# M's scale from a bound on its factors, Wv turned by DMA, two tiles of x turned by TensorE: a two-layer graph kernel on one core

## The chip, the cores and the metric

One core of a Trainium2 chip. The metric is the device time of one execution, in microseconds (us), the median of several runs. Times in the profile are counted from the start of the profiled execution's span.

## The reference, cut to what matters

```python
def reference(x, adj, Wq, bq, Wk, bk, Wv, bv, W1, b1, W2, b2):      # x 4096x512, adj 4096x4096, W* 512x512, W1 512x128
    q, k, v = x @ Wq.T + bq, x @ Wk.T + bk, x @ Wv.T + bv
    a = q @ k.T / sqrt(512) + adj + adj
    x = layernorm(x + softmax(a) @ v)
    h = relu(adj @ (x @ W1) + b1)
    return layernorm(x + adj @ (h @ W2) + b2)
```

## The kernel before, in words

All large products run on TensorE in fp16, each operand split in two: `hi` is the scaled value rounded to fp16 (on ScalarE), `lo` is what is left (on VectorE, `minus_hi`, L1159). A product of two split operands takes three matmuls per block of 128, hi x hi, hi x lo and lo x hi (`terms`, L577, lines 578 to 580), each with 512 columns. The scales are powers of two, taken from maxima or sums of absolute values: VectorE reduces along the free axis, GpSimd takes the maximum over the 128 partitions (`partition_all_reduce`), VectorE rounds to a power (`power`, `scale_of`: four small instructions).

The queries and keys are folded into one matrix. M = Wq' Wk (512 x 512) is made first, in fp32 (line 601), in four PSUM banks `m_bank`. Then the logits are x M x' plus biases: `queries(n)` (L634) makes a 128 x 512 piece of g = M'x' and `values(t)` (L620) a 128 x 512 tile of v. Their order on TensorE is written out at L653 to L662: queries(0) to (3), values(0) to (3), then two of each in turn up to t = 31. Only then come the logits, the softmax and the attention (L665 on, 256 steps of 24 matmuls), and the two convolutions with adj. The change touches nothing of these.

What stands ahead of queries(0), by engine:

- SyncE (SP) issues the loads: the first quarters of Wq and Wk (`d_w0`), their other three (`d_wr`), x group 0 (four tiles of 128 rows, 1 MB), Wv, x group 1. Then it waits, tile by tile, for the split of x and issues a DMA transpose for each of tiles 0 to 3 (`transpose_x`, L362; 256 KB, an fp16 pair, into `xT`), then bv's row, x groups 2 and 3, the transposes of tiles 4 to 7, and x groups 4 to 7. Its waits hold everything behind them.
- TensorE runs nine warm-up matmuls (L595), M (16 products, two instructions each, quarter e = 0 of the weights first), four column sums (L607), c0 (L609), the bias row (L610: ones x part_u, 512 columns, fp32), and 16 transposes of Wv's blocks into PSUM (`wv_transposes`, L588 to L591). queries(0) waits for the four DMA transposes and, block by block, for M's split (`a_m`, `v_m`).
- ScalarE sums |x| of the first half of group 0 (`group_sum`, L849), splits tiles 0 to 3 (`xt_hi`, L858), sums group 1, copies the bias row out of bank 7 (L898, `a_bias`), and makes `m_hi` (L865), `g_hi(0)` (L875) and `wv_hi` (L889) from PSUM.
- VectorE makes `part_u` and `part_g` (`partial`, L1163: Wq's and Wk's rows weighted with the biases), the other half of group 0's sum (L1240), x's scale (`x_scale(0)`, L1186), `xt_lo` (L1182) of tiles 0 to 3, then the maxima over M's banks as they come (`m_max`, L1174), M's scale, the first part of Wv's maximum, `m_lo` (L1208), `g_scale(0)` (L1200), the rest of Wv's maximum, x's second scale, Wv's scale, `wv_lo` (L1178) and the split of tiles 4 to 7.
- GpSimd does the all-reduces in a fixed order (L1572 on) and counts them in `g_ar`.

After that, `g_hi`/`g_lo` scale and split each query piece, `v_full` (L1212), `v_hi` and `v_lo` each tile of v, and `query_bias` (L1280) multiplies x with the bias row. queries(4) to (7) take the banks of queries(0) to (3) again, values(4) to (7) those of values(0) to (3), so they wait for `a_gf` and `v_vf`. The list `x_tiles_at` (L97) says at which tile t the split of a later group of four tiles stands.

## Time and profile before

| | us |
|---|---|
| median of 3 runs | 1907.52 (1907.30 to 1907.54) |
| the profiled execution's own time | 1907.61 |
| its span, first to last instruction | 1905.8 |
| TensorE busy in the span | 1897.2 |
| VectorE, ScalarE, GpSimd busy | 1082.8, 857.4, 116.0 |
| granted TensorE clock, whole span | 1.00 |

The own time is what the device reports for the profiled execution; the span is shorter, as it leaves out what lies before the first and behind the last instruction. Matmuls overlap each other in the profile (each is shown with about 0.38 us, a new one starts every 0.22 us), so starts tell more than durations.

### The profile page before, as it was taken

Reading aid. Unit: us, or ns where it says so; the run is one execution under the profiler, and the core shown is the slowest. Engines: PE = TensorE matmul, PEld = TensorE weight load, DVE = VectorE, ACT = ScalarE, POOL = GpSimd, SP = SyncE. Lnnn points to the kernel's source line nnn. Section 1 sums busy time; section 2 is a strip of 40 time slices with the busy share of each in tenths; the row PEclk is TensorE's granted clock in tenths of the full one; section 3 lists DMA queues with packets and bytes.
Section 4 is the critical chain, followed back from the end, with each engine's and each line's share of the span. In section 5 each row is a group of like instructions: output and inputs, shape, how many; then the busy total and the mean of one; then the engine's idle time right before and its main releaser. Section 6 shows DMA issues by size and latency. Waiting matters only on the chain.

```text
span 1905.8 us, 26547 instructions
## 1 busy us (share of the span) xinstructions
PE 1897.2 (100%) x9273; PEld 889.8 (47%) x9273; DVE 1082.8 (57%) x2107; ACT 857.4 (45%) x1838; POOL 116.0 (6%) x210
## 2 busy tenths in 40 slices
PE   9999999999999999999999999999999999999998
PEld 4444444444444444444444444444444454444446
DVE  7786666666666666666666666666666620001334
ACT  5654455555555455555555555555545611010112
POOL 0000000000000000000000000000000000002334
PEclk9999999999999999999999999999999999999999
DMA  7665599999999999999999999999999999989996
GB/s 234 164 138 123 127 231 227 225 231 227 227 223 226 228 229 228 227 224 226 225 230 225 229 226 231 226 222 226 228 222 237 215 349 387 387 307 358 395 394 244
DMA packets 798903, 463.21 MB, mean 243 GB/s; under 512 B 644656, under 2 KB 652592, under 8 KB 798768
## 3 DMA queue, kind: packets, MB, share of 16 engines
q1 hardware_dynamic: 790704, 447.51, 93.4%
q10 hardware_dynamic: 8064, 14.00, 2.0%
q8 instruction: 73, 1.20, 0.3%
q14 instruction: 62, 0.51, 0.1%
HBM read 220.99 MB, written 92.01 MB: 164 GB/s over the span
## 4 chain that ended last, share of the span: by engine, by line
PE 98%; DVE 1%; DMA 0%; issue 0%; POOL 0%; SPq 0%; ACT 0%; POOLq 0%; DVEq 0%; ACTq 0%
PE bank L578 15%; PE bank L580 15%; PE bank L579 15%; PE bank L690 12%; PE bank L691 12%; PE bank L692 12%; PE bank L814 5%; PE bank L813 5%; PE bank L815 5%; DMA adj_in<-in_L_gnn_Wk 0%; PE bank L777 0%; PE bank L774 0%; PE bank L773 0%; PE bank L834 0%; PE bank L835 0%; PE bank L836 0%
## 5 line engine op out<-in xcount | busy, mean ns | idle before, releaser
L959 ACT ACTIVATE tsp<-ring,sc 128x512 f16<-128x512 f32 x248 | 179.0, 722 | 599.3 <-DMA tsp<-tsp 598.5
L1341 DVE SCALAR_TENSOR_TENSOR ring<-bank,sc,adj_in 128x512 f32<-128x512 f32 x256 | 192.2, 751 | 396.1 <-PE bank L580 391.1
L578 PE MATMUL bank<-xT,gT 128*128 128x512 f16 x1024 | 388.1, 379 | 0.0
L579 PE MATMUL bank<-xT,gT 128*128 128x512 f16 x1024 | 388.1, 379 | 0.0
L580 PE MATMUL bank<-xT,gT 128*128 128x512 f16 x1024 | 388.1, 379 | 0.0
L690 PE MATMUL bank<-xv,tsp 128*128 128x512 f16 x1008 | 382.0, 379 | 0.0
L691 PE MATMUL bank<-xv,tsp 128*128 128x512 f16 x1008 | 382.0, 379 | 0.0
L692 PE MATMUL bank<-xv,tsp 128*128 128x512 f16 x1008 | 382.0, 379 | 0.0
L1160 DVE SCALAR_TENSOR_TENSOR tsp<-adj_in,s_a,tsp 128x512 f16<-128x512 f32 x248 | 184.7, 745 | 48.3 <-ACT tsp L967 47.9
L1160 DVE SCALAR_TENSOR_TENSOR tsp<-ring,sc,tsp 128x512 f16<-128x512 f32 x248 | 184.8, 745 | 0.1
L947 ACT ACTIVATE ring<-ring,bias 128x512 f32<-128x512 f32 x256 | 180.9, 707 | 7.4 <-DVE bias L1358 7.4
L1349 DVE TENSOR_REDUCE r_max<-ring 128x1 f32<-128x512 f32 x256 | 175.7, 686 | 8.8
L967 ACT ACTIVATE tsp<-adj_in,s_a 128x512 f16<-128x512 f32 x248 | 175.1, 706 | 3.9 <-DMA tsp<-tsp 3.6
L935 ACT ACTIVATE junk<-adj_in 128x512 fp8e4<-128x512 f32 x256 | 157.0, 613 | 10.1 <-DMA adj_in<-in_adj 10.0
L579 PEld LDWEIGHTS bank<-xT,gT 128*128 128x128 f16 x1024 | 100.2, 98 | 120.8
L578 PEld LDWEIGHTS bank<-xT,gT 128*128 128x128 f16 x1024 | 100.2, 98 | 120.8
L580 PEld LDWEIGHTS bank<-xT,gT 128*128 128x128 f16 x1024 | 100.2, 98 | 120.8
L692 PEld LDWEIGHTS bank<-xv,tsp 128*128 128x128 f16 x1008 | 98.6, 98 | 118.9
L690 PEld LDWEIGHTS bank<-xv,tsp 128*128 128x128 f16 x1008 | 98.6, 98 | 115.3 <-DMA tsp<-tsp 0.5
L691 PEld LDWEIGHTS bank<-xv,tsp 128*128 128x128 f16 x1008 | 98.6, 98 | 114.8
L1503 DVE TENSOR_TENSOR xv<-bank,xv 128x512 f16<-128x512 f32 x8 | 5.5, 691 | 153.2 <-ACT xv L1048 153.2
L1054 ACT ACTIVATE tsp<-tsp,shift,rstd 128x512 f32<-128x512 f32 x31 | 25.2, 813 | 122.5 <-POOL shift L1618 122.4
(261 smaller groups left out, 2167.3 us busy)
## 6 DMA issues: line engine op xcount, KB each, us to landing
adj_in<-in_adj SPq DMA_DIRECT2D x256, 256.0 KB, 3.2
at_dram<-tsp SPq DMA_DIRECT2D x248, 256.0 KB, 3.2
xv<-at_dram SPq DMA_DIRECT2D x54, 1024.0 KB, 14.5
adj_in<-at_dram SPq DMA_DIRECT2D x29, 1024.0 KB, 14.4
xT<-at_dram SPq DMA_DIRECT2D x20, 1024.0 KB, 13.7
xv<-in_x SPq DMA_DIRECT2D x8, 1024.0 KB, 9.9
g_dram<-tsp SPq DMA_DIRECT2D x32, 256.0 KB, 4.0
...
```

What stands on the lines that cost most here:

```text
L578: pe.matmul(dst, ah, bh, start=first, stop=False)
L579: pe.matmul(dst, ah, bl, start=False, stop=False)
L580: return pe.matmul(dst, al, bh, start=False, stop=last)
L690: pe.matmul(dst, ah, vh, start=(kb == 0 and j == 0), stop=False)
L691: pe.matmul(dst, ah, vl, start=False, stop=False)
L692: last = pe.matmul(dst, al, vh, start=False, stop=(kb == KB - 1 and j == TW - 1))
L947: act.activation(p, p, ACT.Exp, bias=bias[:, r % 2:r % 2 + 1], scale=2.0, accum_out=r_sum[:, r % 2, kb:kb + 1]).then_inc(a_exp, 1)
L959: act.activation(p_split(e)[:, 0:BANK], p, ACT.Copy, scale=col[f"p_up{batch(TW * kb)}"]).then_inc(a_p, 1)
L967: act.activation(asp[a % 2][:, 0:BANK], adj_in[:, a % AR, :], ACT.Copy, scale=s_a[:, r:r + 1]).then_inc(a_ah, 1)
L1160: return dve.scalar_tensor_tensor(dst, src, scale, hi, ALU.mult, ALU.subtract)
L1341: dve.scalar_tensor_tensor(t, s_bank[s % S_BANKS][:, :], col[f"k_l{batch(s // KB)}{batch(TW * (s % KB))}"], adj_in[:, s % AR, :], ALU.mult ...
L1349: dve.tensor_reduce(r_max[:, r % 2, kb:kb + 1], ring[:, s % RING, :], AX, ALU.max).then_inc(v_max, 1)
```

## The change

- **M's scale.** Instead of a maximum over the finished M it takes a bound: for each of the 512 rows, the sum of |Wq| times the maximum of |Wk|, and the largest of these. ScalarE makes the row sums (`row_sum`), VectorE the maxima and their product. The scale is `TOP_M / D` over the bound's power instead of `TOP` over the maximum's. For g's own scale a maximum over the hi half of M (`st_mh`) is taken later. m_hi now waits for each bank by itself.
- **Tiles 2 and 3 of x** are transposed by TensorE in fp32, between M's second and third quarters, into banks 4 and 5, and split from there (`xt_hi_pe`, `xt_lo_pe`). Tiles 0 and 1 stay with the DMA (`X_DMA = 2`).
- **Wv** is split from SBUF, into a part of `xT` that is free until the end, and transposed by four DMA transposes ahead of those of tiles 4 to 7, of bv's row and of x groups 3 to 7; x group 2 goes before them. TensorE's 16 transposes go. Wv's scale comes from sums of |Wv| on ScalarE (over each partition's 2048 values); its maximum is taken later, for v's scale (`st_w`).
- **Order.** part_u is completed behind g_scale(0); the bias row's matmul stands between values(2) and values(3), in bank 0; g_hi(0) to (3) stand behind the split of tiles 4 to 7; the split of tiles 8 to 11 stands at t = 2 instead of t = 4, without a g_hi in its middle.

The diff, cut to its core (the counts in other waits on `g_ar` move by one):

```diff
...
 TOP = 2.0 ** 13
+TOP_M = 2.0 ** 14
...
 def x_tiles_at(t):
 
 
-    return list(range(t + XG, t + 2 * XG)) if t % XG == 0 and 0 < t < NT - XG else []
+    if t == XG - 2:
+        return list(range(2 * XG, 3 * XG))
+    return list(range(t + XG, t + 2 * XG)) if t % XG == 0 and XG < t < NT - XG else []
 
...
-        wv_bank = bank[4:8]
+        wv_split = xT[:, KB - 1, :, :, :].rearrange("p two k n -> p (two k n)").rearrange("p (k two d) -> p k two d", k=KD, two=2)
+        row_sums = c_all[:, 0:KD]
 
         def queries_bank(n):
...
-            for t in range(XS):
+            for t in range(X_DMA):
+                transpose_x(t)
+            load_x(X_FIRST)
+            for k in range(KD):
+                sp.wait_ge(a_wv, k + 1)
+                sp.wait_ge(v_wv, k + 1)
+                sp.dma_start_transpose(wvT.rearrange("p two k e -> p (two k) e")[:, :, P * k:P * (k + 1)],
+                                       wv_split[:, k, :, :].rearrange("p two d -> p (two d)")).then_inc(d_wvt, 16)
+            for t in range(XG, 2 * XG):
                 transpose_x(t)
             sp.dma_start(bv_row, bv.rearrange("(o d) -> o d", o=1).broadcast_to([P, D])).then_inc(d_bv, 16)
-            for i in range(X_FIRST, X_FIRST + 2):
-                load_x(i)
-            for t in range(XG, 2 * XG):
-                transpose_x(t)
-            for i in range(X_FIRST + 2, NT // XG):
+            for i in range(X_FIRST + 1, NT // XG):
...
             for t in range(NT):
                 for q in x_tiles_at(t):
+                    if q == NT - XG:
+                        sp.wait_ge(d_wvt, 16 * KD)
                     transpose_x(q)
                 if t == XG:
...
-            def wv_transposes(j):
-                for k in range(KD):
-                    last = pe.transpose(wv_bank[j][:, P * k:P * (k + 1)], wv_raw[:, k, P * j:P * (j + 1)], ident)
-                last.then_inc(p_wv, 1)
+            def x_transposes_first():
+                pe.wait_ge(d_x[0], 16)
+                pe.wait_ge(g_id, 2)
+                for t in range(X_DMA, XG):
+                    for k in range(KD):
+                        last = pe.transpose(x_bank[t - X_DMA][:, P * k:P * (k + 1)], xv[:, t, P * k:P * (k + 1)], ident)
+                    last.then_inc(p_xt, 1)
...
                 if e == 1:
                     pe.wait_ge(d_wr, 16 * 2)
+                if e == 2:
+                    x_transposes_first()
                 for k in range(KD):
                     last = pe.matmul(m_bank[k][:, :], wq_raw[:, e, P * k:P * (k + 1)], wk_raw[:, e, :],
                                      start=(e == 0), stop=(e == KD - 1))
                     if e == KD - 1:
                         last.then_inc(p_pre, 1)
-            pe.wait_ge(v_part, 3)
+            pe.wait_ge(v_part, 2)
...
             last.then_inc(p_pre, 1)
             pe.matmul(bank[6][:, KD:KD + 1], ones, col["c0p"], start=True, stop=True).then_inc(p_pre, 1)
-            pe.matmul(bank[7][:, :], ones, part_u, start=True, stop=True).then_inc(p_pre, 1)
-            pe.wait_ge(d_wv, 16)
-            pe.wait_ge(g_id, 2)
-            wv_transposes(0)
-            wv_transposes(1)
-            pe.wait_ge(v_gb, 2)
-            wv_transposes(2)
-            pe.wait_ge(a_bias, 1)
-            wv_transposes(3)
+
+            def bias_row():
+                pe.wait_ge(v_part, 3)
+                pe.wait_ge(a_gf, 1)
+                pe.matmul(bank[0][:, :], ones, part_u, start=True, stop=True).then_inc(p_pre, 1)
...
             def values(t):
                 if t >= V_BANKS:
                     pe.wait_ge(v_vf, t - V_BANKS + 1)
-                if t % XG == 0:
+                if t == 0:
+                    pe.wait_ge(d_wvt, 16 * KD)
+                elif t % XG == 0:
                     for i in range(XS):
-                        pe.wait_ge(d_xt[i], 16 * (t // XG + 1))
+                        pe.wait_ge(d_xt[i], 16 * x_transposes(t + i))
+                if t == 2:
+                    pe.wait_ge(v_gb, 2)
                 for k in range(KD):
-                    if t == 0:
-                        pe.wait_ge(a_wv, k + 1)
-                        pe.wait_ge(v_wv, k + 1)
                     last = terms(v_bank[t % V_BANKS][:, :], xt_block(0, k, P * t, P), xt_block(1, k, P * t, P),
                                  wvT[:, 0, k, :], wvT[:, 1, k, :], k == 0, k == KD - 1)
                 last.then_inc(p_v, 1)
...
             def queries(n):
                 g, kk = divmod(n, KD)
                 if kk == 0:
+                    if g == 0:
+                        pe.wait_ge(a_xt, XG)
+                        pe.wait_ge(v_xt, XG)
                     for i in range(XS):
-                        pe.wait_ge(d_xt[i], 16 * (g + 1))
+                        if x_transposes(XG * g + i):
+                            pe.wait_ge(d_xt[i], 16 * x_transposes(XG * g + i))
...
                 elif n >= Q_BANKS:
+                    if n == Q_BANKS:
+                        pe.wait_ge(a_bias, 1)
                     pe.wait_ge(a_gf, n - Q_BANKS + 1)
...
             for n in range(XG):
                 queries(n)
-            for t in range(XG):
+            for t in range(XG - 1):
                 values(t)
+            bias_row()
+            values(XG - 1)
...
+            def row_sum(e):
+                if e:
+                    act.wait_ge(a_rs, e)
+                act.activation(x_junk[:, 0:D], wq_raw[:, e, :], ACT.Abs, accum_out=row_sums[:, e:e + 1], saturate=False).then_inc(a_rs, 1)
...
+            def xt_hi_pe(t):
+                act.wait_ge(p_xt, t - X_DMA + 1)
+                act.activation(xt_pe(0, t), x_bank[t - X_DMA][:, :].rearrange("p (k n) -> p k n", n=P), ACT.Identity,
+                               scale=col["s_x0"]).then_inc(a_xt, 1)
...
             def m_hi(k):
+                act.wait_ge(p_pre, k + 1)
                 act.activation(m_hl[:, 0, k, :], m_bank[k][:, :], ACT.Identity, scale=col["s_m"]).then_inc(a_m, 1)
...
             def wv_hi(k):
-                act.wait_ge(p_wv, k + 1)
-                act.activation(wvT[:, 0, k, :], wv_bank[k][:, :], ACT.Identity, scale=col["s_wv"]).then_inc(a_wv, 1)
-
+                act.activation(wv_split[:, k, 0, :], wv_raw[:, k, :], ACT.Identity, scale=col["s_wv"]).then_inc(a_wv, 1)
+
+            act.wait_ge(d_w0, 16 * 2)
+            row_sum(0)
+            act.wait_ge(d_wr, 16 * 2)
+            for e in range(1, KD):
+                row_sum(e)
+            act.wait_ge(a_rs, KD)
             group_sum(0)
-            for t in range(XS):
+            for t in range(X_DMA):
                 xt_hi(t)
-            group_sum(1)
-            act.wait_ge(p_pre, KD + 3)
-            act.activation(c_row, bank[7][:, :], ACT.Copy).then_inc(a_bias, 1)
+            act.wait_ge(d_wv, 16)
+            act.wait_ge(a_xs, 1)
+            act.activation(x_junk[:, 0:KD * D], flat(wv_raw), ACT.Abs, accum_out=col["t1"], saturate=False).then_inc(a_ws, 1)
+            for t in range(X_DMA, XG):
+                xt_hi_pe(t)
             act.wait_ge(v_sm, 1)
             for k in range(KD):
                 m_hi(k)
-            g_hi(0)
             act.wait_ge(v_sc, 1)
             for k in range(KD):
                 wv_hi(k)
+            act.wait_ge(a_ws, 1)
+            group_sum(1)
             for t in range(XG, 2 * XG):
                 xt_hi(t)
-            for n in range(1, XG):
+            group_sum(X_FIRST)
+            for n in range(XG):
                 g_hi(n)
-            group_sum(X_FIRST)
+            act.wait_ge(p_pre, KD + 3)
+            act.activation(c_row, bank[0][:, :], ACT.Copy).then_inc(a_bias, 1)
+            group_sum(X_FIRST + 1)
...
                 for i, q in enumerate(x_tiles_at(t)):
-                    if i == 2:
+                    if i == 2 and t >= XG:
...
-            def wv_max(i, rows):
-                link(abs_max(col[f"t{i}"], flat(wv_raw[:, rows, :])))
-
-            def m_max(k):
-                dve.wait_ge(p_pre, k + 1)
-                link(abs_max(col[f"m{k}"], m_bank[k][:, :]))
...
             def wv_lo(k):
                 dve.wait_ge(a_wv, k + 1)
-                minus_hi(wvT[:, 1, k, :], wv_bank[k][:, :], col["s_wv"], wvT[:, 0, k, :]).then_inc(v_wv, 1)
+                minus_hi(wv_split[:, k, 1, :], wv_raw[:, k, :], col["s_wv"], wv_split[:, k, 0, :]).then_inc(v_wv, 1)
...
+            def xt_lo_pe(t):
+                dve.wait_ge(a_xt, t + 1)
+                hi, lo = (xT[:, 0, part, :, P * t:P * (t + 1)] for part in range(2))
+                minus_hi(lo, x_bank[t - X_DMA][:, :].rearrange("p (k n) -> p k n", n=P), col["s_x0"], hi).then_inc(v_xt, 1)
...
-                link(dve.tensor_scalar(col["k_g"], col[f"e_x{b}"], col["e_m"], LOGIT / TOP ** 2, ALU.mult, ALU.mult))
-                link(dve.tensor_scalar(col["bound"], col["k_g"], 4.0 * TOP ** 2, col["mx_gb"], ALU.mult, ALU.add))
+                link(dve.tensor_scalar(col["k_g"], col[f"e_x{b}"], col["e_m"], LOGIT * D / (TOP * TOP_M), ALU.mult, ALU.mult))
+                link(dve.tensor_scalar(col["bound"], col["k_g"], col["mx_mh"], col["mx_gb"], ALU.mult, ALU.add))
...
             partial(part_g, wk_raw, bq_c, 0)
             link(dve.tensor_tensor(bqk[:, :], bq_c[:, :], bk_c[:, :], ALU.mult))
             dve.tensor_reduce(col["c0p"], bqk[:, :], AX, ALU.add).then_inc(v_part, 1)
+            link(abs_max(col["m0"], wk_raw[:, 0, :]))
             dve.wait_ge(d_wr, 16 * 2)
-            for e in range(1, KD - 1):
-                partial(part_u, wq_raw, bk_c, e)
-                partial(part_g, wk_raw, bq_c, e)
+            link(abs_max(cols("m1", "m3"), wk_raw[:, 1:KD, :]))
+            partial(part_g, wk_raw, bq_c, 1)
             dve.wait_ge(d_x[0], 16)
             dve.tensor_reduce(x_sum[:, 1:2], flat(xv[:, XG // 2:XG, :]), AX, ALU.add, apply_absolute_value=True).then_inc(v_st, 1)
-            partial(part_u, wq_raw, bk_c, KD - 1)
+            partial(part_g, wk_raw, bq_c, 2)
             x_scale(0)
+            dve.wait_ge(a_rs, KD)
+            link(dve.tensor_tensor(cols("m0", "m3"), cols("m0", "m3"), row_sums, ALU.mult))
+            dve.tensor_reduce(col["t0"], cols("m0", "m3"), AX, ALU.max).then_inc(v_st, 1)
+            for t in range(X_DMA):
+                xt_lo(t)
+            dve.wait_ge(g_ar, 2)
+            power(col["e_m"], col["e_m"], TINY_M)
+            scale_of(col["s_m"], col["e_m"], TOP_M / D).then_inc(v_sm, 1)
             partial(part_g, wk_raw, bq_c, KD - 1)
-            for t in range(XG):
-                xt_lo(t)
+            for t in range(X_DMA, XG):
+                xt_lo_pe(t)
+            dve.wait_ge(v_sm, 1)
+            m_lo(0)
+            dve.wait_ge(g_ar, 3)
+            power(col["e_wv"], col["e_wv"])
+            scale_of(col["s_wv"], col["e_wv"]).then_inc(v_sc, 1)
+            for k in range(1, KD):
+                m_lo(k)
+            dve.wait_ge(v_sc, 1)
             for k in range(KD):
-                m_max(k)
-            dve.tensor_reduce(col["st_m"], cols("m0", "m3"), AX, ALU.max).then_inc(v_st, 1)
+                wv_lo(k)
             dve.wait_ge(p_pre, KD + 2)
             dve.tensor_scalar(gb_c[:, :], bank[6][:, 0:KD], LOGIT, None, ALU.mult).then_inc(v_gb, 1)
             dve.tensor_scalar(col["c0"], bank[6][:, KD:KD + 1], LOGIT, None, ALU.mult).then_inc(v_gb, 1)
             dve.wait_ge(v_gb, 2)
-            abs_max(col["st_gb"], gb_c[:, :]).then_inc(v_st, 1)
-            dve.wait_ge(g_ar, 3)
-            power(col["e_m"], col["mx_m"])
-            scale_of(col["s_m"], col["e_m"]).then_inc(v_sm, 1)
-            dve.wait_ge(d_wv, 16)
-            wv_max(0, slice(0, 1))
-            dve.wait_ge(v_sm, 1)
-            for k in range(KD):
-                m_lo(k)
-            dve.wait_ge(g_ar, 4)
-            g_scale(0)
-            wv_max(1, slice(1, KD))
-            dve.tensor_reduce(col["st_wv"], cols("t0", "t1"), AX, ALU.max).then_inc(v_st, 1)
+            link(abs_max(col["st_gb"], gb_c[:, :]))
+            abs_max(col["st_mh"], m_hl[:, 0, :, :].rearrange("p k e -> p (k e)")).then_inc(v_st, 1)
             x_scale(1)
-            dve.wait_ge(g_ar, 5)
-            power(col["e_wv"], col["mx_wv"])
-            scale_of(col["s_wv"], col["e_wv"]).then_inc(v_sc, 1)
-            g_lo(0)
-            dve.wait_ge(v_sc, 1)
-            for k in range(KD):
-                wv_lo(k)
             for t in range(XG, 2 * XG):
                 xt_lo(t)
+            dve.wait_ge(g_ar, 5)
+            link(dve.tensor_scalar(col["mx_mh"], col["mx_mh"], 2.002 * TOP, None, ALU.mult))
+            g_scale(0)
+            for e in range(1, KD):
+                partial(part_u, wq_raw, bk_c, e)
+            g_lo(0)
             g_lo(1)
+            abs_max(col["st_w"], flat(wv_raw)).then_inc(v_st, 1)
             dve.wait_ge(d_bv, 16)
             link(abs_max(col["mx_bv"], bv_row))
-            v_scale(0)
             def query_bias(t):
                 dve.wait_ge(d_x[t // XG], 16)
                 dve.tensor_tensor_reduce(unused, xv[:, t, :], c_row, 1.0, 0.0, ALU.mult, ALU.add, c_all[:, t:t + 1]).then_inc(v_c, 1)
 
             dve.wait_ge(a_bias, 1)
             query_bias(0)
+            dve.wait_ge(g_ar, 6)
+            link(dve.tensor_scalar(col["mx_w"], col["mx_w"], 2.0, None, ALU.mult))
+            v_scale(0)
...
+            pool.wait_ge(v_st, 2)
+            pool.partition_all_reduce(col["e_m"], col["t0"], P, ALL_MAX).then_inc(g_ar, 1)
+            pool.wait_ge(a_ws, 1)
+            pool.partition_all_reduce(col["e_wv"], col["t1"], P, ALL_MAX).then_inc(g_ar, 1)
             pool.wait_ge(a_xs, 2)
             pool.partition_all_reduce(x_all[:, X_COLUMNS[1]], x_sum[:, X_COLUMNS[1]], P, ALL_MAX).then_inc(g_ar, 1)
-            pool.wait_ge(v_st, 2)
-            pool.partition_all_reduce(col["mx_m"], col["st_m"], P, ALL_MAX).then_inc(g_ar, 1)
             pool.wait_ge(v_st, 3)
-            pool.partition_all_reduce(col["mx_gb"], col["st_gb"], P, ALL_MAX).then_inc(g_ar, 1)
+            pool.partition_all_reduce(cols("mx_gb", "mx_mh"), cols("st_gb", "st_mh"), P, ALL_MAX).then_inc(g_ar, 1)
             pool.wait_ge(v_st, 4)
-            pool.partition_all_reduce(col["mx_wv"], col["st_wv"], P, ALL_MAX).then_inc(g_ar, 1)
+            pool.partition_all_reduce(col["mx_w"], col["st_w"], P, ALL_MAX).then_inc(g_ar, 1)
...
```

## Rows read from the trace of the kernel before

**Rows 1.** The page, busy time by engine, share of the span, instructions.

```profile
PE 1897.2 (100%) x9273; PEld 889.8 (47%) x9273; DVE 1082.8 (57%) x2107; ACT 857.4 (45%) x1838; POOL 116.0 (6%) x210
```

**Rows 2.** Busy time by stretch; columns: stretch, length, engines, granted clock, DMA share, GB/s.

```profile
0.00:25.20 25.20, 22.69 (x78) 13.38 (x79) 15.68 (x35) 9.19 (x13) 2.64 (x13) 1.00 0.81 255
25.20:46.00 20.80, 20.79 (x97) 9.24 (x98) 19.72 (x50) 15.87 (x24) 0.75 (x2) 1.00 0.70 200
...
240.00:1500.00 1260.00, 1260.00 (x6097) 581.85 (x6096) 806.99 (x1499) 660.31 (x1506) 40.92 (x60) 1.00 1.02 227
```

**Rows 3.** The chain that ended last, in order of time: start, us, what.

```profile
23.30 0.17 DVE sc L1157
...
24.31 0.76 DVE ring L1160
25.07 0.14 issue
...
224.86 0.39 PE bank L690
```

**Rows 4.** SP's timeline: the first four DMA transposes; and transposes' time to landing.

```profile
17.39 2.71 SPq L366 DMA_TRANSPOSE xT<-ring  x2
20.19 1.29 SPq L366 DMA_TRANSPOSE xT<-x1s  x1
21.57 1.29 SPq L366 DMA_TRANSPOSE xT<-w_hl  x1
...
DMA to landing us min/median/max: 3.1/3.2/3.3
```

**Rows 5.** Timeline of TensorE ahead of queries(0): start, us, line, out<-in.

```profile
9.55 0.30 PEld L601 LDWEIGHTS bank<-adj_in 128*128 128x128 f32 x2 [0.91 <-DMA adj_in<-in_L_gnn_Wk]
...
19.96 0.95 PE L607 MATMUL bank<-tsp 128*128 128x1 f32 x8
...
20.99 1.10 PE L610 MATMUL bank<-tsp 128*128 128x512 f32 x2
21.93 1.91 PE L590 MATMUL bank<-junk,adj_in 128*128 128x128 f32 x16
25.21 0.38 PE L578 MATMUL bank<-xT,ring 128*128 128x512 f16 x1 [1.36 <-DVE ring L1160]
```

**Rows 6.** ScalarE's timeline, ahead of values(0) and, last, in the attention.

```profile
12.27 1.06 ACT L855 ACTIVATE gT<-xv 128x1024 fp8e4<-128x1024 f32 x1 [9.34 <-DMA xv<-in_x]
...
15.79 1.33 ACT L863 ACTIVATE ring<-xv,sc 128x512 f16<-128x512 f32 x2 [2.37 <-DVE sc L1157]
...
18.26 1.89 ACT L855 ACTIVATE gT<-xv 128x2048 fp8e4<-128x2048 f32 x1
...
28.72 0.78 ACT L882 ACTIVATE adj_in<-bank,gb_s,sc 128x512 f32<-128x512 f32 x1 [2.81 <-DVE gb_s L1206]
29.53 0.63 ACT L887 ACTIVATE tsp<-adj_in 128x512 f16<-128x512 f32 x1
...
1002.18 0.61 ACT L935 ACTIVATE junk<-adj_in 128x512 fp8e4<-128x512 f32 x1
```

**Rows 7.** VectorE's timeline in the same stretch.

```profile
12.69 1.22 DVE L1240 TENSOR_REDUCE x_sum<-xv 128x1 f32<-128x1024 f32 x1
...
15.60 0.15 DVE L1157 TENSOR_SCALAR sc<-sc 128x1 f32<-128x1 f32 x1
...
24.31 2.73 DVE L1160 SCALAR_TENSOR_TENSOR ring<-bank,sc,ring 128x512 f16<-128x512 f32 x4 [0.26 <-ACT ring L866]
...
26.95 0.20 DVE L1201 TENSOR_SCALAR sc<-sc 128x1 f32<-128x1 f32 x1
...
28.54 1.75 DVE L1149 TENSOR_REDUCE sc<-adj_in 128x1 f32<-128x1536 f32 x1
```

**Rows 8.** GpSimd's timeline: the first all-reduce.

```profile
14.13 0.67 POOL L1572 PARTITION_ALL_REDUCE x_all<-x_sum  x1 [12.18 <-DVE x_sum L1240]
```

**Rows 9.** DMA issues in 16 to 27 us: KB each, median us to landing.

```profile
xv<-in_x SPq DMA_DIRECT2D x2, 1024.0 KB, 8.8
```

More of the change, by code:

```diff
@@ L22 @@
 XS = 4
+X_DMA = 2
 X_FIRST = 2
@@ L46 @@
 TOP = 2.0 ** 13
+TOP_M = 2.0 ** 14
 TINY = 2.0 ** -40
+TINY_M = 2.0 ** -62
 EXP_BITS = 0x7F800000
@@ L215, in gnn_program @@
         minus_mean = sb("minus_mean", [P, O_RING], F32)
-        names = ["m0", "m1", "m2", "m3", "st_wv", "st_w1", "mx_wv", "mx_w1", "e_wv", "e_w1", "s_wv", "s_w1",
-                 "st_m", "st_gb", "mx_m", "mx_gb", "e_m", "s_m", "mx_bv", "c0p", "c0", "t0", "t1", "u0", "u1", "bound",
+        names = ["m0", "m1", "m2", "m3", "st_w1", "mx_w1", "e_wv", "e_w1", "s_wv", "s_w1",
+                 "st_gb", "st_mh", "st_w", "mx_gb", "mx_mh", "mx_w", "e_m", "s_m", "mx_bv", "c0p", "c0", "t0", "t1", "u0", "u1", "bound",
                  "mx_x", "e_x0", "s_x0", "k_v0", "e_v0", "s_v0", "k_g", "e_g0", "s_g", "k_gs0", "p_up0",
@@ L261, in gnn_program @@
         v_row = [tsp[:, 8, :].bitcast(F32), adj_in[:, 9, :]]
-        g_rows = [adj_in[:, first + i, :] for first in (2, 10) for i in range(2)]
+        g_rows = [adj_in[:, first + i, :] for first in (4, 10) for i in range(2)]
         unused = gT[:, 1, 0:D].bitcast(BF16)
@@ L290, in gnn_program @@
         m_bank = bank[0:4]
+        x_bank = bank[4:6]
         def g_row(n):
@@ L314, in gnn_program @@
             sem(s) for s in ("d_small", "d_bv", "d_w1", "d_b1", "d_wv", "d_late"))
+        d_wvt = sem("d_wvt")
         d_w0, d_wr = sem("d_w0"), sem("d_wr")
@@ L328, in gnn_program @@
         d_out = [sem(f"d_out{i}") for i in range(O_RING)]
-        p_wv, p_pre, p_v, p_g, p_qk, p_pv, p_y, p_adj, p_x1, p_unit, p_h, p_o, p_end = (
-            sem("p_" + s) for s in "wv pre v g qk pv y adj x1 unit h o end".split())
+        p_xt, p_pre, p_v, p_g, p_qk, p_pv, p_y, p_adj, p_x1, p_unit, p_h, p_o, p_end = (
+            sem("p_" + s) for s in "xt pre v g qk pv y adj x1 unit h o end".split())
+        a_rs, a_ws = sem("a_rs"), sem("a_ws")
         a_w2, v_w2, v_z, v_o = sem("a_w2"), sem("v_w2"), sem("v_z"), sem("v_o")
@@ L860, in xt_hi, with xt_pe @@
                     act.wait_ge(v_sx, batch(t) + 1)
-                if t >= XS:
-                    act.wait_ge(d_xt[t % XS], 16 * (t // XS))
+                if t >= XS and x_transposes(t - XS):
+                    act.wait_ge(d_xt[t % XS], 16 * x_transposes(t - XS))
                 act.activation(x_split[t % XS][:, 0:D], xv[:, t, :], ACT.Identity, scale=col[f"s_x{batch(t)}"]).then_inc(a_xt, 1)
+            def row_sum(e):
+                if e:
+                    act.wait_ge(a_rs, e)
+                act.activation(x_junk[:, 0:D], wq_raw[:, e, :], ACT.Abs, accum_out=row_sums[:, e:e + 1], saturate=False).then_inc(a_rs, 1)
+            def xt_pe(part, t):
+                return xT[:, 0, part, :, P * t:P * (t + 1)]
+            def xt_hi_pe(t):
+                act.wait_ge(p_xt, t - X_DMA + 1)
+                act.activation(xt_pe(0, t), x_bank[t - X_DMA][:, :].rearrange("p (k n) -> p k n", n=P), ACT.Identity,
+                               scale=col["s_x0"]).then_inc(a_xt, 1)
             def m_hi(k):
+                act.wait_ge(p_pre, k + 1)
                 act.activation(m_hl[:, 0, k, :], m_bank[k][:, :], ACT.Identity, scale=col["s_m"]).then_inc(a_m, 1)
@@ L920, in _ @@
                 v_hi(t)
-                if X_FIRST + 1 + t < NT // XG:
-                    group_sum(X_FIRST + 1 + t)
+                if 2 <= t < NT // XG - X_FIRST:
+                    group_sum(X_FIRST + t)
             for i in range(XS):
-                act.wait_ge(d_xt[i], 16 * len(range(i, NT, XS)))
+                act.wait_ge(d_xt[i], 16 * x_transposes(NT - XS + i))
             act.wait_ge(v_scales, 1)
@@ L983, in x1_hi @@
                     for i in range(XS):
-                        act.wait_ge(d_xt[i], 16 * len(range(i, NT, XS)))
+                        act.wait_ge(d_xt[i], 16 * x_transposes(NT - XS + i))
                 act.activation(x1s[:, 0:D], xr[:, :], ACT.Copy, scale=X1_UP).then_inc(a_x1, 1)
@@ L1293, in _ @@
                         x_scale(batch(q))
-                    if i == 2:
+                    if i == 2 and t >= XG:
                         g_lo(t)
@@ L1323, in _ @@
                 if t == NT // 2 + 4:
-                    dve.wait_ge(g_ar, 8)
+                    dve.wait_ge(g_ar, 9)
                     power(col["e_w1"], col["mx_w1"])
```

16 lines of the change are left out of this document (9 added, 7 removed).

## The prediction

> **What bounds the kernel now.** I read the busy times by engine first: TensorE is busy for 1897.2 of the span's 1905.8 us [rows 1]. Then the busy time by stretch [rows 2]: in 0 to 25.2 us TensorE has 22.69 us, in 25.2 to 46.0 it has 20.79 of 20.80, in 240 to 1500 it has all of 1260, and the granted clock is 1.00 in each, the 2.4 GHz level. So the only place where a change at the start can win is the idle time and the order of work before the first three-term product, which starts at 25.21. The 20.8 us behind it hold eight products (queries(0) to (3), values(0) to (3)) of twelve matmuls, 2.60 us each; queries(4) starts at 25.21 + 8 x 2.60 = 46.01. That start is the number to predict: from there on the same products follow in the same order.
>
> The chain of waits says what ends last [rows 3]: m_lo(0) on VectorE from 24.31, 0.14 us of issue after its end at 25.07, then queries(0). Behind it stand the four maxima over the M banks, one all-reduce and the scale. But a second wait ends almost together with it: the transposes of x's first four tiles are issued at 17.39, about 18.8, 20.19 and 21.57 and land 3.1 to 3.3 us after issue [rows 4], the last at 21.57 + 3.2 = 24.8. Removing M's maxima alone would win 0.3 us. And TensorE's own queue ends with M's product, four small sums, c0, the bias row and 16 transposes of Wv, from 21.93 for 1.91 us [rows 5]. All three have to move; the change moves all three.
>
> **VectorE and ScalarE ahead of M's scale.** ScalarE gets four row sums of Wq. One costs 0.61 us plus its accumulator read, 0.7 to 0.8 with the wait between (the adj sums in [rows 6] are of that shape). Three follow the weights at 9.55: done by 11.9, ahead of x group 0, which releases ScalarE at 12.27 [rows 6]. So they cost nothing; without that cover each would push s_x0 by 0.8. On VectorE a maximum over 1536 elements (1.75 us [rows 7]) takes the place of two partial sums of 0.76, part_u goes behind, and x_sum can start at 12.3 instead of 12.69 [rows 7]. s_x0, ready at 15.75 before (the multiply at 15.60 is its last step), comes at 15.35 (x_sum to 13.5, 0.2 to GpSimd, all-reduce 0.67 [rows 8], then five small steps of 0.19, the pace of [rows 3]). The product of sums and maxima takes two more small steps; its all-reduce is over by 16.6 and hides beside xt_hi and xt_lo of tiles 0 and 1. xt_lo(1) is done at 17.5 and s_m at 18.2, over 5 us before its old time of 23.45.
>
> ScalarE: xt_hi(0), (1) 15.4 to 16.7 (1.33 for two [rows 6]); the sum over 2048 elements of Wv 16.6 to 18.6 (1.89 + 0.19 read, by group_sum(1)'s row); two PSUM passes for tiles 2 and 3 to 19.9; then m_hi(0), whose bank has been ready since 18.5, 19.8 to 20.5. VectorE: part_g's last term to 18.9, xt_lo_pe of tiles 2 and 3 19.35 to 20.8, m_lo(0) 20.7 to 21.45, four small steps for s_wv to 22.1, m_lo(1), (2), (3) ending at 22.8, 23.45 and 24.1 (0.66 us apart [rows 7]).
>
> **TensorE.** 24 instructions from 9.55 to 19.96 make M's last three quarters, 0.43 us each, 0.87 a product [rows 5]. Eight fp32 transposes now stand inside: 1.91/16 = 0.12 each, 0.95 in all. M ends at 20.9; the sums and c0 take 20.99 - 19.96 = 1.03 as before: free at 21.95. queries(0) also needs m_lo(0) (21.45 + 0.15 = 21.6), xt_lo_pe(3) (20.8) and the DMAs of tiles 0 and 1 (issued at 16.95 and 18.3, landed 21.5). TensorE's own queue ends last, with 0.35 us between the three. Inside queries(0) each quarter takes 0.65, and m_lo(1) at 22.8 + 0.1 holds the second by 0.3; the last starts at 24.2. It ends at 24.87 against 27.83 before: **2.95 us gained**.
>
> **Values.** queries(1) to (3) end at 32.67. values(0) now waits for four DMA transposes of Wv's split. wv_hi runs on ScalarE 22.1 to 24.7, wv_lo on VectorE 24.0 to 26.8, each 0.66 apart, first pair at 24.8. SP waits on each pair; behind it stand x tiles 4 to 7, bv's row and x groups 3 to 7. Issue is at 24.85 and then every 1.38 us (that of [rows 4]): the last at 29.0, landed at 32.2. **0.5 us of slack, the thinnest of the change.** From both sides: with landing at 3.1 and x2 out of the way it is 32.1; if the first Wv transpose finds x group 2 in the queue, it can be late. Group 2 is issued at 19.65; a 1 MB group took 8.8 us to land where two were issued among transposes [rows 9], so 28.5 is the far end. I take 32.2, since only two transposes (to 21.5) stand before a single megabyte.
>
> On that place a rule speaks: the transposes of [rows 4] keep 1.38 us between issues for 256 KB, 190 GB/s. The Trainium skill (Advanced Engine Details and Errata, X-Bar Transpose) says that transposing DMAs are as fast as plain ones, 350 to 400 GB/s. By it, as an estimate from that figure, Wv's four would land at about 30: over 2 us of slack, rival (b) all but gone, the sum the same. The trace disagrees, and I go by the trace.
>
> **The bias row and queries(4).** values(0) to (2) end at 40.47. bias_row, once in the idle stretch, now stands between values(2) and (3): two fp32 instructions, 21.93 - 20.99 = 0.94 us [rows 5], **lost in full**. It waits for part_u and g_hi(0). VectorE after wv_lo: maximum over M's 2048 fp16 (no such row; 1.75 x 2048/1536 = 2.3, from 1.2 if two bytes go twice as fast) to 29.4, s_x1 30.3, xt_lo(4) to (7) to 33.8, g_scale(0) (26.95 to 28.54 is 1.6 [rows 7]) to 35.5, part_u's three terms to 37.8: 2.6 before 40.47. g_hi(0) gives its bank back at 36.5. bias_row ends at 41.4, values(3) at **44.0**. queries(4) needs the copy of the row out of bank 0, on ScalarE behind g_hi(0) to (3): 35.65 + 4 x 1.35 (0.76 + 0.63 [rows 6]), with 0.2 of waiting for g_lo, is 41.2; the row is in by 41.55, copied 42.15, slack 1.8. Tiles 4 to 7 are issued from 31.9 to 36.0 and land at 39.2, slack 4.8.
>
> Next in line is values(4) at 49.2, which wants v_full(0). VectorE: g_lo(1) to 39.1, Wv's maximum 2.3 to 41.4, bv (issued 37.3, 5 us at worst) 42.3 to 43.0, query bias, v_scale(0) 1.3 (six small steps), g_lo(2), v_full(0) done at 46.5: slack 2.7. The third group's split at t = 2 then needs x group 3 (issued 37.9, landed 46.7 by the 8.8 us) and its sum at 48.7; VectorE comes there at 50.6. v_full(2) at 55 for values(6) at 59.6; tiles 8 to 11 land at 60.4 for queries(8) at 64.8. All hidden.
>
> **The sum.** 46.01 - 44.0 = **2.0 us** less: 2.95 gained, 0.94 given back. TensorE has no other waits to take it up: the only odd step later is 0.2 us at 224.86 [rows 3], and everything up to there moves with TensorE. The profiled execution's own time is 1907.61, span 1905.8; the median of the runs is 1907.52. 1907.55 - 2.05 gives **1905.5**.
>
> **The rivals.** (a) The thin waits are late by a little: Wv's transposes, a_bias, or m_lo(1) cost 0.5 to 2 us in all. For it: three starts lie within 0.5 us, and my steps carry 0.1 us errors a dozen times over. Against it: all else has over 1.8. Result 1906.0 to 1907.5. (b) Slower: Wv's transposes queue behind x group 2 at values(0). With group 2 landing at 28.5 the four follow at 1.38, the last landing at 28.5 + 3 x 1.38 + 3.2 = 35.8, 3.1 us after values(0) could start: 1905.5 + 3.1 = 1908.6. It decides from a landing later than 32.67 + 2.0 = 34.7. Against it: alone in the queue a megabyte is through in some 3 us. (c) More gained: M's quarters without the stall of m_lo(1), and the 0.2 us at 224.86 gone: 1905.0. (d) The change doesn't do what it says: s_m late, as the scale waits for row sums or the all-reduce. It has 1.6 us before m_hi(0) wants it, and with the old order of events kept but the bias row and DMA waits added it would be 1907.5 to 1908.5.
>
> **How the numbers follow.** The forecast (1904.9 to 1906.0) 0.60, (a) 0.22, (b) 0.07, (c) 0.06, (d) 0.05. The range of 8 in 10 takes the forecast, (c)'s upper part and (a) up to 1907.1. A measurement of this kernel tells 0.2%, 3.8 us, from no change: faster wants a start of queries(4) before 42.2, which the bias row and TensorE's own queue exclude (0.02). Slower wants the landing of (b) 5.9 us beyond need, or several waits of over 2.6 us (0.04). The rest, 0.94, is within 0.2%.
>
> **What would show it.** In the trace after: the first matmul of queries(0) at 22.0 with next to no idle time before it; 16 transposes gone, eight inside M's product; a gap of 0.3 inside queries(0); none before values(0); the bias row's 0.94 us before values(3); queries(4) at 44.0. Wrong if values(0) shows a DMA wait, if queries(0) starts after 23, or if a gap appears before queries(4) or values(4).

## The result and the profile after

The change makes the kernel **slower by 5.4 us**: 1912.74 us (median of 8 runs, 1912.17 to 1913.86) against 1907.32 (8 runs, 1907.10 to 1907.54), ratio 1.0029, interval 1.0018 to 1.0040. The forecast was 1905.5 and no measurable change. The profiled execution took 1912.83, with a span of 1910.9.

The start of the trace is within 0.3 us of the forecast. TensorE's timeline after, at queries(0), the bias row, queries(4), and at queries(12) (start, us, line, out<-in; an idle time before and its releaser in brackets):

```profile
20.50 0.95 PE L633 MATMUL bank<-tsp 128*128 128x1 f32 x8
21.31 0.36 PE L635 MATMUL bank<-sc,tsp 128*128 128x1 f32 x2
21.61 0.38 PE L599 MATMUL bank<-xT,ring 128*128 128x512 f16 x1
...
40.27 1.02 PE L640 MATMUL bank<-tsp 128*128 128x512 f32 x2
41.13 0.38 PE L599 MATMUL bank<-ring,xT 128*128 128x512 f16 x1
...
43.72 0.38 PE L599 MATMUL bank<-xT,ring 128*128 128x512 f16 x1
...
84.94 0.38 PE L601 MATMUL bank<-ring,xT 128*128 128x512 f16 x1
89.94 0.59 PE L599 MATMUL bank<-xT,ring 128*128 128x512 f16 x1 [4.61 <-ACT adj_in L927]
90.31 0.63 PE L600 MATMUL bank<-xT,ring 128*128 128x512 f16 x1
```

queries(0), the last row of [rows 5], starts at 21.61 instead of 25.21. queries(4) starts at 43.72; the kernel before starts it at 45.96 by the same view, so 2.24 us are won there, and they are still there at 84.94. Then queries(12) starts at 89.94, where 84.94 + 0.22 = 85.16 was due: **4.78 us lost in one wait**. And the matmuls behind it are 0.43 us apart instead of 0.22. Busy time by stretch, in the columns of [rows 2] (TensorE's busy time is the third figure; granted clock, DMA share and GB/s are the last three):

```profile
84.00:86.00 2.00, 1.32 (x7) 0.39 (x4) 2.00 (x4) 0.65 (x2) 0.00 (x0) 1.00 1.04 194
86.00:88.00 2.00, 0.00 (x0) 0.00 (x0) 1.81 (x5) 0.72 (x1) 0.00 (x0) 1.00 0.95 184
88.00:90.00 2.00, 0.07 (x1) 0.10 (x2) 1.71 (x4) 1.58 (x3) 0.00 (x0) 0.53 1.01 205
90.00:92.00 2.00, 2.00 (x5) 0.64 (x6) 0.89 (x2) 1.74 (x3) 0.00 (x0) 0.50 0.94 215
92.00:94.00 2.00, 2.00 (x6) 0.76 (x5) 1.82 (x5) 0.72 (x1) 0.00 (x0) 0.50 0.91 209
94.00:96.00 2.00, 2.00 (x8) 0.79 (x7) 1.96 (x4) 0.61 (x1) 0.00 (x0) 0.76 0.00 0
```

The granted clock goes from 1.00 to 0.50 (2.4 to 1.2 GHz) while TensorE stands still, and the matmuls are 0.22 us apart again from 94.99 on. The twelve starts from 89.94 to the next at 94.99 take 5.05 us instead of 2.59: another 2.46. The account: -2.24 + 4.78 + 2.46 = +5.0; the spans differ by 5.1.

Who is late? The profile puts the wait down to ScalarE's g_hi (L927), but queries(12) also waits for the DMA transposes of tiles 12 to 15. SP's timeline after, and below it what the transposes' own view says of their landing and of who waited:

```profile
82.37 2.63 SPq L381 DMA_TRANSPOSE xT<-ring  x2
85.09 1.29 SPq L381 DMA_TRANSPOSE xT<-x1s  x1
86.47 1.28 SPq L381 DMA_TRANSPOSE xT<-w_hl  x1
```

```profile
  PEld bank L599: 5.1, 1
...
DMA to landing us min/median/max: 3.2/3.2/3.3
```

Tile 15 lands at 86.47 + 3.2 = 89.7, and TensorE starts at 89.94. The same view of the kernel before:

```profile
78.36 2.60 SPq L366 DMA_TRANSPOSE xT<-ring  x2
81.05 1.28 SPq L366 DMA_TRANSPOSE xT<-x1s  x1
82.43 1.29 SPq L366 DMA_TRANSPOSE xT<-w_hl  x1
```

There tile 15 landed at 82.43 + 3.2 = 85.6, and queries(12) started at 87.40: about 1.8 us of slack, at a place that neither the diff nor the waits of TensorE point to. After, TensorE comes 2.24 earlier and the last issue 4.0 later. ScalarE's timeline after shows where most of the 4.0 come from:

```profile
59.70 1.89 ACT L886 ACTIVATE gT<-xv 128x2048 fp8e4<-128x2048 f32 x1
61.50 0.19 ACT L886 ACTIVATION_READ_ACCUMULATOR gT<-xv 128x1 f32 x1
61.59 0.76 ACT L927 ACTIVATE adj_in<-bank,gb_s,sc 128x512 f32<-128x512 f32 x1
...
68.89 1.89 ACT L886 ACTIVATE gT<-xv 128x2048 fp8e4<-128x2048 f32 x1
70.69 0.19 ACT L886 ACTIVATION_READ_ACCUMULATOR gT<-xv 128x1 f32 x1
70.78 0.76 ACT L927 ACTIVATE adj_in<-bank,gb_s,sc 128x512 f32<-128x512 f32 x1
```

and VectorE's, its g_lo at those two places:

```profile
63.12 0.69 DVE L1281 TENSOR_TENSOR tsp<-adj_in,tsp 128x512 f16<-128x512 f32 x1 [1.34 <-ACT tsp L932]
...
72.24 0.69 DVE L1281 TENSOR_TENSOR tsp<-adj_in,tsp 128x512 f16<-128x512 f32 x1 [2.47 <-ACT tsp L932]
```

These are the sums of |x| of x groups 5 and 7. The diff ahead of the prediction does not show the lines that put them there:

```diff
                 v_hi(t)
-                if X_FIRST + 1 + t < NT // XG:
-                    group_sum(X_FIRST + 1 + t)
+                if 2 <= t < NT // XG - X_FIRST:
+                    group_sum(X_FIRST + t)
```

With `X_FIRST` = 2 the sums of groups 4 to 7 move from t = 1 to 4 to t = 2 to 5 (group 3's moves from t = 0 to ahead of the loop). Sums 5 and 7, at t = 3 and t = 5, now stand right ahead of g_hi(4) and g_hi(6). VectorE waits for each g, and the values behind it wait too: v_full(4) starts at 64.98 instead of 62.98, v_full(6) at 74.17 instead of 70.28.

### The profile page after: what moved, and what is told of

It reads as the page before. It is cut to its first block, busy times and chain, and to the rows that moved or that the text cites. A ratio compares the mean times of both kernels' runs of the same rounds, so it can differ in the third digit from the quotient of the medians.

```text
span 1910.9 us, 26546 instructions
## 1 busy us (share of the span) xinstructions
PE 1898.7 (99%) x9265; PEld 889.4 (47%) x9265; DVE 1085.5 (57%) x2107; ACT 862.2 (45%) x1848; POOL 116.4 (6%) x211
## 4 chain that ended last, share of the span: by engine, by line
PE 94%; DVE 2%; ACT 1%; DMA 1%; issue 1%; SPq 0%; POOL 0%; POOLq 0%; DVEq 0%; ACTq 0%
PE bank L599 14%; PE bank L600 14%; PE bank L601 14%; PE bank L721 12%; PE bank L722 12%; PE bank L723 12%; PE bank L845 5%; PE bank L844 5%; PE bank L846 5%; DMA xv<-in_x 0%; PE bank L808 0%; PE bank L805 0%; PE bank L804 0%; PE bank L866 0%; PE bank L865 0%
```

## The experiments

Three theories of why the split of tiles 12 to 15 is late. **A**: these two sums. **B**: the values' chain starts too late (v_full(0) at 45.26 instead of 42.12; bv's row and two maxima over 2048 elements stand ahead of it) and never catches up. **C**: the split of tiles 8 to 11 at t = 2 pushes the later one. And the clock: does it fall because of the wait?

All are edits of the changed kernel. Times are medians of eight to eleven runs, the last two columns are from the one profiled execution (in f_sum7 and e_warm this was the slowest of its ten, at 1910.45 and 1911.76); the kernel before ran beside them at 1907.2. "Last issue" is SP's last transpose of tiles 12 to 15, "idle" TensorE's idle time right before queries(12).

| run | edit | us | last issue | idle |
|---|---|---|---|---|
| the change | | 1912.74 | 86.47 | 4.61 |
| e_sums | sums 4 to 7 at t = 2, 4, 6, 8 | 1906.39 | 82.78 | 0.43 |
| f_sum7 | sum 7 at t = 6 | 1909.65 | 85.09 | 2.33 |
| e_bv | bv's load before Wv's transposes | 1911.98 | 85.53 | 4.18 |
| e_t4 | tiles 8 to 11 at t = 4 | 1910.38 | 86.61 | 0.25, and 2.53 before queries(8) |
| f_t6 | tiles 12 to 15 at t = 6 | 1906.45 | 76.09 | none |
| e_warm | matmuls in the wait | 1910.43 | 87.33 | filled |
| f_best | sums, bv and t = 6 together | 1905.58 | 71.85 | none |

**The sums.**

```diff
-                if 2 <= t < NT // XG - X_FIRST:
-                    group_sum(X_FIRST + t)
+                if t % 2 == 0 and 2 <= t < 10:
+                    group_sum(X_FIRST + 1 + t // 2)
```

> The changed kernel with x's group sums 4 to 7 on ScalarE behind v_hi of t = 2, 4, 6, 8 instead of t = 2, 3, 4, 5. Theory A (the sums at t = 3 and t = 5 stand right ahead of g_hi(4) and g_hi(6), 1.9 us each; VectorE waits for these, and with it the split and the DMA transposes of tiles 12 to 15 come 3.8 us later, behind the start of queries(12)): the last transpose of tile 15 lands near 85.9 instead of 89.7, TensorE waits 1 us or less before queries(12) instead of 4.6, the granted clock stays at 1.00, and the time falls from 1912.7 to 1905.2 to 1906.2. Theory B (the chain of the values starts 3 us too late, bv's load and the two maxima over 2048 elements being in front of it): the wait before queries(12) stays over 3 us and the time over 1911. Theory C (the split of tiles 8 to 11 at t = 2 is what pushes the later one): the same as B.

Measured 1906.39 (1905.98 to 1907.01), ratio to the kernel before 0.9996 (0.9987 to 1.0005). The last issue moves by 3.7 us, as A has it; TensorE waits 0.43 us, and the clock stays up (the second row is a stretch, in the columns of [rows 2]):

```profile
86.17 0.38 PE L599 MATMUL bank<-xT,ring 128*128 128x512 f16 x1 [0.43 <-DMA xT<-w_hl]
...
84.00:88.00 4.00, 3.57 (x18) 1.49 (x16) 2.72 (x6) 3.94 (x7) 0.38 (x1) 1.00 0.98 208
```

Here the wait is named as what it is, the DMA into `xT`. The time is 0.2 us above A's range; this execution also waited 0.50 us for Wv's transposes before values(0). **6.3 us of the change's time hang on where the sums stand.** (The edit also moves sum 6, which stood ahead of no g_hi.) Next, half of the edit, only sum 7 moved:

```diff
-                if 2 <= t < NT // XG - X_FIRST:
-                    group_sum(X_FIRST + t)
+                if t in (2, 3, 4, 6):
+                    group_sum(X_FIRST + min(t, 5))
```

> The changed kernel with only x's group sum 7 moved, from t = 5 (right ahead of g_hi(6)) to t = 6; sums 4, 5 and 6 stay at t = 2, 3, 4. A dose: if each sum that stands right ahead of a g_hi costs 1.9 us, the DMA transposes of tiles 12 to 15 come 1.9 us earlier than in the changed kernel, TensorE waits about 2.7 us before queries(12) instead of 4.6, the clock still falls, and the time is 1910.0 to 1911.5. If the lateness is worked off in another way (both sums together, or the first alone), it is near 1906.4 or 1912.7.

1909.65 (1907.66 to 1910.45): near the range, 0.35 us below it. The last issue came 1.4 us earlier. The idle time fell by 2.3, more than that, as TensorE itself came 0.8 later in this execution (it was idle for 0.73 us ahead of values(0), against 0.16 in the change). The clock still fell to 0.50. Three of the ten runs were at 1907.66, 1907.70 and 1907.96; whether the clock held in these was not profiled.

**The place of the splits.**

```diff
-    if t == XG - 2:
-        return list(range(2 * XG, 3 * XG))
-    return list(range(t + XG, t + 2 * XG)) if t % XG == 0 and XG < t < NT - XG else []
+    return list(range(t + XG, t + 2 * XG)) if t % XG == 0 and 0 < t < NT - XG else []
```

> The changed kernel with the split of tiles 8 to 11 back at t = 4, with g_hi(4) and g_lo(4) in its middle, as in the kernel before. Theory C (the place at t = 2 is to blame): the wait before queries(12) is gone, about 1905. Theory A: g_hi(4) now stands in the middle of the split, where ScalarE's sum of t = 3 is hidden behind x's third scale, so one of the two sums' 1.9 us goes; the other stays: a wait of 2 to 3 us before queries(12), 1908 to 1910. Theory B: little changes, 1911 to 1913. The last transpose of tile 11 must then also land before queries(8) at about 64: 62.85 + 3.2 in the kernel before would be too late by 1 to 2 us for it, a new wait in every theory.

1910.38 (1908.81 to 1911.85). The new wait came, 2.53 us before queries(8), and took the clock down with it:

```profile
67.21 0.58 PE L597 MATMUL bank<-xT,ring 128*128 128x512 f16 x1 [2.53 <-DMA xT<-w_hl]
```

That delay brought TensorE to queries(12) late enough to wait only 0.25 there, although the last issue was at 86.61, no earlier than in the change. So C, which had the wait gone and 1905, falls as the whole cause. But the last issue hides a part of it. The split of tile 15 on VectorE, first in the change, then in e_t4, and SP's first two transposes of the group in e_t4:

```profile
84.14 0.74 DVE L1216 SCALAR_TENSOR_TENSOR w_hl<-xv,sc,w_hl 128x512 f16<-128x512 f32 x1
82.95 0.75 DVE L1214 SCALAR_TENSOR_TENSOR w_hl<-xv,sc,w_hl 128x512 f16<-128x512 f32 x1
81.18 3.95 SPq L379 DMA_TRANSPOSE xT<-ring  x2
```

With the old place VectorE had the split 1.2 us earlier, and SP lost that again: its two issues took 3.95 us instead of 2.63. Why is not known. The place at t = 2 thus has a share of 1.2 us in VectorE's lateness; what it would be worth in time no run shows. The move to t = 2 is still the part of the change that queries(8) needs. A's 2 to 3 us at queries(12) were not seen either, since the loss at queries(8) hid them. The other way round, tiles 12 to 15 earlier as well:

```diff
+    if t in (XG - 2, 2 * XG - 2):
+        return list(range(t + XG + 2, t + 2 * XG + 2))
+    return list(range(t + XG, t + 2 * XG)) if t % XG == 0 and 2 * XG < t < NT - XG else []
```

> The changed kernel with the split and the transposes of tiles 12 to 15 at t = 6 instead of t = 8, g_hi(6) in their middle; the group sums stay where the change has them. If nothing but the landing of tile 15 holds queries(12), it lands some 5 us or more earlier, the wait is gone and the time is 1905.0 (the 2.5 us gained ahead of queries(4) stay, and nothing is lost). If queries(12) is held by something else (the bank's release by g_hi, the profile's ACT L927), the wait stays at over 3 us and the time at 1911 or more.

1906.45 (1906.12 to 1906.82): the wait before queries(12) is gone, so the landing of tile 15 and not the bank held it, and the profile's "ACT adj_in L927" was not the cause. (e_warm below says the same: its extra matmuls also wait for that bank, and start without a gap.) The time is 1.4 us above my figure. Part of that is a wait one group later (tiles 16 to 19 at t = 12, 0.51 us):

```profile
106.54 0.38 PE L599 MATMUL bank<-xT,ring 128*128 128x512 f16 x1 [0.51 <-DMA xT<-w_hl]
```

**bv's row.**

```diff
             load_x(X_FIRST)
+            sp.dma_start(bv_row, bv.rearrange("(o d) -> o d", o=1).broadcast_to([P, D])).then_inc(d_bv, 16)
             for k in range(KD):
...
-            sp.dma_start(bv_row, bv.rearrange("(o d) -> o d", o=1).broadcast_to([P, D])).then_inc(d_bv, 16)
```

> The changed kernel with bv's row loaded right behind x group 2, ahead of Wv's DMA transposes, instead of behind the transposes of tiles 4 to 7. VectorE's wait for it (0.86 us ahead of 41.81) goes. Theory B (the late start of the values' chain sets the lateness at tiles 12 to 15): everything on VectorE from 41.8 on comes 0.9 us earlier, the wait before queries(12) falls from 4.6 to about 3.7 and the time by 0.9 to 2 us. Theory A: VectorE meets the g pieces anyway at t = 4 and t = 6 where ScalarE's sums hold it, so less than 0.5 us is seen.

1911.98 (1911.0 to 1913.02), 0.8 less; the last issue came 0.94 earlier. B's 0.9 us for VectorE is right and A's "less than 0.5" wrong: VectorE does carry a delay from 42 us through to 82. The idle time fell by only 0.43, as TensorE also came 0.44 earlier, and the 0.8 us of time are just under B's range, with the two kernels' runs overlapping (1912.17 to 1913.86 in the change). B's part is 0.9 of lateness, the sums' 3.7, so A is the larger. No run has these two edits alone together; with t = 6 in both, f_best has its last issue 4.2 us ahead of f_t6's, near their sum.

**The clock.**

```diff
+                if n == 3 * XG:
+                    pe.wait_ge(a_gf, n - Q_BANKS + 1)
+                    for _ in range(22):
+                        pe.matmul(queries_bank(n)[:, :], m_hl[:, 0, 0, 0:P], xt_block(0, 0, 0, BANK), start=True, stop=True)
```

> The changed kernel with 22 matmuls of 512 columns on old data in TensorE's queue ahead of queries(12), into the bank that queries(12) overwrites: they only fill the wait (22 x 0.216 = 4.75 us against 5.0 between the starts around it). If the half clock of the first eleven matmuls of queries(12) comes from the wait before it, the clock stays 1.00, these matmuls start every 0.216 us instead of 0.43 and 2.4 us are gained: 1910.2. If the clock fell for another reason (a fixed time, the load), the time stays at 1912.7.

1910.43 (1909.94 to 1911.76), 2.3 less. The matmuls start right behind the last of values, and the clock is 1.00 in the stretch that had 0.50:

```profile
86.52 4.91 PE L662 MATMUL bank<-xT,ring 128*128 128x512 f16 x22
...
88.00:92.00 4.00, 4.00 (x20) 1.84 (x19) 3.25 (x6) 2.69 (x4) 0.00 (x0) 1.00 0.97 200
```

So the wait itself took the clock down, and the loss divides into the 4.8 of the wait and about 2.4 of the clock behind it.

**All repairs, and what each move at the start is worth.** Sums, bv and t = 6 in one kernel:

> All three repairs on the changed kernel: tiles 12 to 15 split at t = 6, the group sums behind even tiles, bv's row loaded ahead of Wv's transposes. Every wait of TensorE behind 22 us should be gone but the 0.3 of the first attention step: 25.2 - 21.6 = 3.6 us gained at the start, 0.9 given to the bias row: 1904.6 to 1905.2, 2.3 us below the kernel before.

1905.58 (1905.17 to 1906.18), ratio to the kernel before 0.9992 (0.9983 to 1.0001); span 1903.6 against 1905.8. No wait of TensorE over 0.4 us is left behind queries(0)'s start. The gain is 1.7 us by medians and 2.2 by spans, a little less than I expected, and within what this measurement can tell from nothing. On this kernel I undid the three moves one at a time. What the three cost (6.5, 5.6 and 1.2 us) does not add up to the gain of 1.7: they work on waits that end together ahead of queries(0), so each alone, undone, holds back the others' gain too, and in two of them the fall of the clock comes on top. M's scale held back until the four maxima over the banks are done (its value stays the bound's):

```diff
-            dve.tensor_reduce(col["t0"], cols("m0", "m3"), AX, ALU.max).then_inc(v_st, 1)
             for t in range(X_DMA):
                 xt_lo(t)
-            dve.wait_ge(g_ar, 2)
-            power(col["e_m"], col["e_m"], TINY_M)
-            scale_of(col["s_m"], col["e_m"], TOP_M / D).then_inc(v_sm, 1)
             partial(part_g, wk_raw, bq_c, KD - 1)
             for t in range(X_DMA, XG):
                 xt_lo_pe(t)
+            for k in range(KD):
+                dve.wait_ge(p_pre, k + 1)
+                link(abs_max(col["u0"], m_bank[k][:, :]))
+            dve.tensor_reduce(col["t0"], cols("m0", "m3"), AX, ALU.max).then_inc(v_st, 1)
+            dve.wait_ge(g_ar, 2)
+            power(col["e_m"], col["e_m"], TINY_M)
+            scale_of(col["s_m"], col["e_m"], TOP_M / D).then_inc(v_sm, 1)
```

> The kernel with all three repairs, and M's scale held back until VectorE has gone over the four finished banks of M with its maximum, as in the kernel before (the values stay those of the bound). Its price by the rows: the last bank is done at 21.1, maximum to 21.9, all-reduce, power and scale to 23.2, m_hi and m_lo of block 0 to 24.8: queries(0) starts at 24.9 instead of 21.6, 3.3 us later. So the bound is worth 3.3 us: 1908.2. TensorE then stands still for 3 us ahead of queries(0), as no transposes of Wv fill it: if its clock falls, another 2 us: 1910. If the other two moves alone made the start earlier, the bound is worth nothing: 1904.9.

1912.10 (1911.13 to 1912.49): 6.5 us above f_best, and 2.1 above my figure with the clock's fall. queries(0) starts at 26.11, 4.5 later and not 3.3, and its clock is down:

```profile
26.11 0.59 PE L599 MATMUL bank<-xT,ring 128*128 128x512 f16 x1 [4.75 <-DVE ring L1216]
```

Most of the other 1.2 us is this edit's own queue: the four maxima run on VectorE one behind the other from 20.12 to 22.98, where I had the last end at 21.9 (in the kernel before it ends at 22.06). So 4.5 is an upper figure for the bound alone.

x's tiles 2 and 3 by DMA again (`X_DMA = 4`):

> The kernel with all three repairs (1905.6), and x's tiles 2 and 3 transposed by DMA again (four DMA transposes at the start, none of x on TensorE). M ends 0.9 us earlier, but the fourth DMA transpose is issued at 16.7 + 3 x 1.38 = 20.8 and lands at 24.1, so queries(0) starts at 24.1 instead of 21.6: 2.5 us. TensorE is without work for 3 us before it; the granted clock has fallen after waits of 2.5 and 4.6 us and not after 1.4 and 0.5, so I expect it to fall here, for another 2.4 us: 1910.5. If the clock holds: 1908.1. If the two tiles were not needed: 1905.6.

1911.16 (1909.84 to 1911.92), 5.6 above f_best, 0.7 above the branch with the clock's fall: queries(0) at 24.33 after 3.14 us of idle time, then fourteen matmuls 0.43 apart. Wv's transposes back in TensorE's queue, their results unused:

```diff
+            pe.wait_ge(d_wv, 16)
+            for j in range(KD):
+                for k in range(KD):
+                    pe.transpose(bank[7][:, P * k:P * (k + 1)], wv_raw[:, k, P * j:P * (j + 1)], ident)
```

> The kernel with all three repairs, and Wv's 16 transposes put back into TensorE's queue ahead of queries(0), as idle work (their results are not used; the values still come through the DMA). 16 x 0.12 = 1.9 us more in the queue; the 0.2 to 0.4 us of waiting at the first two quarters of queries(0) are filled by it: queries(0) starts at 23.2 to 23.5, 1.5 to 1.7 us lost: 1907.1 to 1907.3, the time of the kernel before. That is what moving Wv to the DMA is worth. If another wait ended queries(0)'s start anyway, the time stays at 1905.6.

1906.76 (1906.48 to 1907.06), 1.2 above f_best and 0.3 below my range, with queries(0) at 23.50. That is 1.9 later than in f_best, less 0.4 of waiting inside queries(0) that it fills.

## Why the prediction was wrong, point by point

- **Right: the front up to queries(4).** Forecast and trace: queries(0) at 21.95 and 21.61; M's quarters, the eight transposes and the sums, free at 21.95 and 21.6; Wv's transposes first issued at 24.85 and 24.34; the maximum over 2048 fp16 2.3 and 2.29 us; bias row 0.94 and 0.86; queries(4) at 44.0 and 43.72. The sum of 2.0 us was 2.24 in the trace: 3.4 gained, 0.3 lost at values(0), 0.86 at the bias row.
- **Wrong by a little: values(0).** The prediction gave it 0.5 us of slack and named a wait there as a sign of being wrong. It waited 0.16 us in the change, 0.50 in e_sums, 0.73 in f_sum7 and 1.47 in e_warm. The second of Wv's transposes was issued 2.27 us behind the first, where 1.38 was counted; the prediction had said that it could find x group 2 in the queue. Rival (b) needed over 2 us and did not come.
- **Wrong: "All hidden."** The step that failed is the end of the part on queries(4). I followed VectorE and ScalarE to v_full(2), gave queries(8) 4.4 us of slack (tiles 8 to 11 landed at 57.29 + 3.2 = 60.5, as forecast), and stopped. The next group, tiles 12 to 15 for queries(12), was not costed, because neither its place at t = 8 nor its code is in the diff. In the trace before it had 1.8 us of slack, less than the 2.24 that TensorE was about to win. By this count it had to be late by some 0.4 us even with nothing else changed. In e_sums it was idle for 0.43, in part by luck: there the last issue came 0.35 later than in the kernel before, and TensorE 0.4 later than in the change.
- **Wrong: the group sums cost nothing.** The prediction used only that of x group 3, ahead of t = 0, for x's third scale; the four behind it, which the change moves by one t, stand in no sum. Each is 1.9 us on ScalarE, and at t = 3 and t = 5 the next thing in its queue is a g_hi for which VectorE waits. e_sums measures it: 3.7 us of lateness, 6.3 us of time.
- **Too small: the late start.** I had v_full(0) done at 46.5 with 2.7 us of slack for values(4), which was right for that wait (it ended at 46.00), and took the delay as absorbed there. e_bv shows that 0.9 us of it are still there at tiles 12 to 15.
- **Wrong: "TensorE has no other waits to take it up."** That TensorE never waited in the trace before says nothing of how nearly it did. And the price of a wait was taken as its length; the fall of the clock behind it added half as much again.
- The point from which I let a case turn slower, a wait of 5.9 us, was too far by the clock's share: 4.8 us of waiting and 2.5 of clock made the 7.2 us between the forecast and the result.
